# Decoder layer, one core: the low parts of the projected context made by GpSimd instead of VectorE, and three biases folded elsewhere

## The reference

```python
# 1: relative-position attention over T=8, 16 heads of 32
qkv = x @ in_proj_weight.T + in_proj_bias             # q, k, v
p = (pos @ pos_proj_weight.T + pos_proj_bias)         # per head
ac = einsum('tbhd,sbhd->bhts', q + r_w_bias, k)
bd = rel_shift(einsum('tbhd,rhd->bhtr', q + r_r_bias, p))[..., :t]
ctx = einsum('bhts,sbhd->tbhd', softmax((ac + bd) / sqrt(32)), v)
x = layernorm(x + ctx @ out_proj_weight.T + out_proj_bias)
# 2: cross attention, 8 heads of 64, over 512 context rows of width 1024
src_key, src_val = split((context @ W_src.T + b_src) * mask)
tgt = (x @ W_tgt.T + b_tgt) * mask
attn = softmax(where(mask == 0, -inf, tgt . src_key / 8))
x = layernorm(x + cat([x, attn . src_val]) @ W_out.T + b_out)
# 3: feed forward 512 -> 2048 -> 512 with values rounded to fp8/fp16
x = layernorm(x + quantized_ffn(x))
```

## Time and profile before

| | us |
|---|---|
| median of 3 runs | 1931.64 (1931.17 to 1934.32) |
| the profiled execution, its own time | 1929.76 |
| its span on the core | 1927.9 |
| first half | 0 to 820 |

### The profile page before, as it was taken

The page is one execution under the profiler, slowest core; times in us unless marked ns, Lnnn a source line. Parts: engine busy times, 40 slices in busy tenths (PEclk is TensorE's granted clock), DMA queues, the critical chain, the costliest instruction groups (busy, mean ns, idle before and its releaser), DMA issues. The chain is left out here.

```text
span 1927.9 us, 33302 instructions
## 1 busy us (share of the span) xinstructions
PE 1829.5 (95%) x12476; PEld 1003.3 (52%) x12476; DVE 1333.2 (69%) x1676; ACT 785.3 (41%) x1208; POOL 558.7 (29%) x576
## 2 busy tenths in 40 slices
PE   7999999999999989878899999999999999999998
PEld 3665465546554646445455454455454554554543
DVE  2899998999899998667465554655655646556521
ACT  3423222222222222248365363562653635626522
POOL 3135964786368345400102002003011020030010
PEclk9999999999999999979999999999999999999999
DMA  8436355425633566574413406207135052071010
GB/s 212 124 79 151 78 152 143 116 77 151 150 94 99 125 172 137 150 167 157 99 39 61 122 1 116 66 1 138 44 51 131 1 111 72 1 133 27 12 33 22
DMA packets 322654, 183.97 MB, mean 95 GB/s; under 512 B 225584, under 2 KB 278832, under 8 KB 322511
## 3 DMA queue, kind: packets, MB, share of 16 engines
q1 hardware_dynamic: 316448, 178.37, 38.9%
q10 hardware_dynamic: 6062, 3.49, 0.8%
HBM read 94.75 MB, written 33.55 MB: 67 GB/s over the span
## 5 line engine op out<-in xcount | busy, mean ns | idle before, releaser
L1531 DVE TENSOR_TENSOR p_lo<-k,p_hi 128x1024 f16<-128x1024 f32 x128 | 156.8, 1225 | 194.4 <-ACT p_hi L1404 194.4
L1176 POOL TENSOR_TENSOR q<-q,x_hi 128x512 f16<-128x512 f32 x28 | 37.6, 1374 | 638.7 <-ACT x_hi L1457 638.7
L1576 DVE CUSTOM_DVE_ANT_0 junk<-b_sx,mneg 128x512 f16<-128x512 f32 x256 | 175.9, 687 | 32.6 <-issue 23.2
L1204 PE MATMUL b_ff<-x2T_hi,w1T_hi 128*128 128x512 f16 x512 | 194.7, 380 | 1.9 <-DVE x2T_lo L1531 1.9
L1204 PE MATMUL b_ff<-x2T_lo,w1T_hi 128*128 128x512 f16 x512 | 194.7, 380 | 0.0
L1204 PE MATMUL b_ff<-x2T_hi,w1T_lo 128*128 128x512 f16 x512 | 194.6, 380 | 0.0
L1436 ACT ACTIVATE k<-b_st,mbias 128x512 f32<-128x512 f32 x256 | 161.9, 685 | 14.0 <-PE b_st L1250 13.4
L577 PE MATMUL sm_b<-cT_hi,wsT_hi 128*128 128x256 f16 x512 | 141.8, 277 | 15.2 <-DMA cT_lo<-rows_lo 13.6
L784 DVE TENSOR_TENSOR prod<-q,k 128x4096 f32<-128x4096 f32 x32 | 142.2, 4443 | 17.5 <-ACT q L660 16.7
L1404 ACT ACTIVATE p_hi<-k 128x1024 f16<-128x1024 f32 x128 | 135.3, 1057 | 45.5 <-PE b_av L1265 43.1
L1428 ACT ACTIVATE hq<-b_ff,b 128x512 fp8e4<-128x512 f32 x128 | 88.0, 687 | 155.6 <-PE b_ff L1204 149.0
(11 more groups left out here) (272 smaller groups left out, 4368.9 us busy)
## 6 DMA issues: line engine op xcount, KB each, us to landing
cn<-in_ctx_dram SPq DMA_DIRECT2D x64, 256.0 KB, 3.1
k<-kT_scratch SPq DMA_DIRECT2D x24, 512.0 KB, 7.7
x<-in_x_dram SPq DMA_DIRECT2D x32, 256.0 KB, 3.1
x_scratch<-x SPq DMA_DIRECT2D x32, 256.0 KB, 2.2
q<-x_scratch SPq DMA_DIRECT2D x8, 1024.0 KB, 5.6
q<-x_scratch SPq DMA_DIRECT2D x32, 256.0 KB, 2.9
out_dram<-q SPq DMA_DIRECT2D x32, 256.0 KB, 4.4
xn<-in_x_dram SPq DMA_DIRECT2D x24, 256.0 KB, 2.9
```

Of the source, the lines that this page charges most:

```text
L1204: mm = pe.matmul(out, a, c, start=(start and n == 0), stop=end)
L1531: dve.tensor_tensor(dst, bank, hi, ALU.subtract).then_inc(out, 1)
L1576: dve.tensor_tensor_reduce(junk[:, :], sx_b[tt % 2][:, :], mneg[:, :], 1.0, NEG, ALU.add, ALU.max, mx[:, h % 2, tt:tt + 1]).then_inc(s["sx ...
```

## The change

1. **Low parts of the context's quarters.** ACT makes two copies of each quarter in place of one: the fp16 high part as before, and the same scaled values in 32 bits (`stage_f`). PE's bank is free after ACT's second copy (`sm_copied`). POOL makes the low part from the two SBUF copies (over the first half of the 32-bit buffer); the instruction of DVE is gone. In POOL's program it stands behind the `o` row and ahead of the `x` and `c` rows of the step.
2. **Bias of k.** The 32 bias matmuls of the k projections are gone. The bias of k enters the position terms: `kb` holds it per head, is multiplied with q's biases in `position_bias` (8 small matmuls in place of 4) and added to `pb` before `position_weights`. Two more loads of a bias as a column at the start, small additions by DVE.
3. **Bias of the context's values.** The 32 bias matmuls of the value quarters are gone. At the start of the second half 12 matmuls with the value bias (`bv16`, 2 rows x 512 columns each) multiply it with the output weights, and DVE adds the result to the output bias. PE does them ahead of the first queries and waits for DVE's `step` to reach 7; one more load of 512 single elements is issued by ACT ahead of its copies.
4. Small things of the first half move into `ctx1`; `ones` is smaller; the first k projection no longer waits for the bias rows, the first q projection does.

```diff
@@ phase_a, buffers
-    stage = [pair(f"stage{i}", [P, 512]) for i in range(2)]
+    stage_f = [sb(f"stage{i}_f", [P, 512], F32) for i in range(2)]
+    stage = [[sb(f"stage{i}_hi", [P, 512], F16)[:, :], stage_f[i][:, :].bitcast(F16)[:, 0:512]] for i in range(2)]
@@ gpsimd
+            def stage_lo(n):
+                hi, lo = stage[n % 2]
+                pool.wait_ge(s["sm_copied"], n + 1)
+                pool.tensor_tensor(lo, stage_f[n % 2][:, :], hi, ALU.subtract).then_inc(s["sm_lo"], 1)
...
                 for use in plan.uses(g):
-                    row_lo(*use)
+                    if use[0] == "o":
+                        row_lo(*use)
+                for n in plan.quarters(g - 1):
+                    stage_lo(n)
+                for use in plan.uses(g):
+                    if use[0] != "o":
+                        row_lo(*use)
@@ tensor
             def position_bias():
-                pe.wait_ge(s["pb_ready"], 4)
+                pe.wait_ge(s["pb_ready"], 8)
                 for o in range(4):
-                    mm = pe.matmul(pos_b[0:2, 128 + o * 64:128 + (o + 1) * 64], bqr2[:, o, :],
-                                   pb[:, o, :, :].rearrange("p h r -> p (h r)"), start=True, stop=True)
+                    for z, terms_of in enumerate((pb, kb)):
+                        mm = pe.matmul(pos_b[0:2, 128 + o * 64:128 + (o + 1) * 64], bqr2[:, z, o, :],
+                                       terms_of[:, o, :, :].rearrange("p h r -> p (h r)"), start=(z == 0),
+                                       stop=(z == 1))
...
-                if (kind, i) == ("k", 0):
+                if (kind, i) == ("q", 0):
                     pe.wait_ge(s["step"], 5)
-                pe.matmul(out, ones, bias, start=False, stop=True).then_inc(s["pj_filled"], 1)
+                if kind != "k":
+                    mm = pe.matmul(out, ones, bias, start=False, stop=True)
+                mm.then_inc(s["pj_filled"], 1)
...
             def context_products(n):
                 if n >= 3:
-                    pe.wait_ge(s["sm_lo"], n - 2)
+                    pe.wait_ge(s["sm_copied"], n - 2)
...
-                    mm = pe.matmul(out[:, :], pick[:, BIAS["src_v"] + 1, :], rows[:, :], start=False, stop=True)
@@ scalar, stage_hi
-                act.activation(stage[n % 2][0][:, :], sm_b[n % 3][:, :], ACT.Copy, scale=scale).then_inc(s["sm_hi"], 1)
+                act.activation(stage[n % 2][0], sm_b[n % 3][:, :], ACT.Copy, scale=scale)
+                act.activation(stage_f[n % 2][:, :], sm_b[n % 3][:, :], ACT.Copy, scale=scale).then_inc(s["sm_copied"], 1)
@@ vector
-            def stage_lo(n):
-                scale = mks[(n // 4) % 2][:, n % 4 - 2:n % 4 - 1] if n % 4 >= 2 else 1.0 / WS
-                hi, lo = stage[n % 2]
-                dve.wait_ge(s["sm_hi"], n + 1)
-                dve.scalar_tensor_tensor(out=lo[:, :], in0=sm_b[n % 3][:, :], scalar=scale, in1=hi[:, :],
-                                         op0=ALU.mult, op1=ALU.subtract).then_inc(s["sm_lo"], 1)
@@ phase_b, tensor
             pe.wait_ge(s["wq_lo"], len(jobs))
+            pe.wait_ge(s["step"], 7)
+            products(ff_b[0][0:2, :], [t for j in range(KT) for t in terms([z[:, j, :] for z in bv16],
+                                                                           [z[:, KT + j, :] for z in wxT])],
+                     None, s["step"])
             queries_and_first_scores(0, None)
@@ phase_b, scalar
+                act.dma_start(bv[:, :], d.src_b[E:2 * E].rearrange("(o p) -> p o", p=P)).then_inc(s["cols_ld"], 16)
@@ phase_b, vector
             dve.tensor_scalar(raw[:, :], raw[:, :], WS, None, ALU.mult).then_inc(s["step"], 1)
-            dve.wait_ge(s["step"], 3)
+            for z in range(2):
+                dve.tensor_copy(bv16[0][:, :, z], bv[:, :]).then_inc(s["step"], 1)
+            dve.wait_ge(s["step"], 5)
+            for z in range(2):
+                dve.tensor_tensor(bv16[1][:, :, z], bv[:, :], bv16[0][:, :, z], ALU.subtract).then_inc(s["step"], 1)
+            dve.wait_ge(s["step"], 8)
+            dve.tensor_tensor(raw[:, :], raw[:, :], ff_b[0][0:2, :], ALU.add).then_inc(s["step"], 1)
```

More of the change, by code:

```diff
@@ L530, in projection @@
                     rhs = [z[:, :, a * E:(a + 1) * E] for z in winT]
-                    ones, bias, out = pick[:, BIAS[kind], :], rows[:, :], pj_b[n % 3][:, :]
+                    ones, bias, out = None if kind == "k" else pick[:, PICK[kind], :], rows[:, :], pj_b[n % 3][:, :]
                 if i == 0:
@@ L557, in output_projection @@
                         pe.matmul(out, a, c, start=(j == 0 and m == 0), stop=False)
-                pe.matmul(out, pick[:, BIAS["out"], :], rows[:, :], start=False, stop=True).then_inc(s["om_filled"], 1)
+                pe.matmul(out, pick[:, PICK["out"], :], rows[:, :], start=False, stop=True).then_inc(s["om_filled"], 1)
             def context_products(n):
@@ L806, in softmax @@
                 dve.tensor_tensor(flat, flat, wide, ALU.subtract).then_inc(s["probs"], 1)
-                for part in plan.quarters(16 * b + 7):
-                    stage_lo(part)
                 dve.wait_ge(s["exped"], b + 1)
@@ L919, in _ @@
                     position_bias()
-                for n in plan.quarters(g - 1):
-                    stage_lo(n)
                 score_sums(0, g)
```

68 lines of the change are left out of this document (41 added, 27 removed).

## The result

The kernel before ran at 1931.4 us in this comparison, the changed kernel at a median of 1952.7 us (1945.6 to 1960.5): the ratio is 1.0109, with a 95% interval of 1.0069 to 1.0149. The forecast was 1924.4 us with a range up to 1940, so the change is slower where a gain was expected. The profiled execution of the changed kernel took 1945.61 us (span 1943.8) and is the shortest of the four; its times are read against the 1929.76 us (span 1927.9) of before, 15.9 us apart.

What follows compares the result with a forecast made beforehand. PE was taken as the bound of the first half, DVE a close second. Terms -13.5 + 1.5 + 0 + 4.8 = -7.2 us from 1931.64 gave 1924.4 us; range 1912.5 to 1940.

Steps and rivals of the forecast that it cites:

- POOL's low part: First half: 64 new POOL instructions, contending with DVE and delaying `c` rows, cost +1.5 us, bounds -9 and +15.
- in value steps the `c` rows come one to two instructions later, 1.15 to 2.3 us: POOL's queue in value steps: low parts ahead of the `c` rows delay them by 1.15 to 2.3 us each time.
- DVE gets 71 us back, so it should still stay behind PE: First half: DVE's 71 us of relief outweighs up to 64 x 1.0 us of contention with POOL.
- POOL paces: Rival, last batch's value steps: POOL's work exceeds PE's 13.3 us a step, costing 15 us; 1938 us, chance 0.20.
- Bias matmuls: First half: 64 fewer bias matmuls on PE, a few small ones added; net -13.5 us if PE stays the bound.
- The relief of DVE: First half: DVE loses 44.7 us of work and 26.3 us of waits, which pays nothing directly.
- its rival at -9: Rival: most of PE's last-batch holes and part of its 13.6 us of waits close, -9 us; 1914 us, chance 0.12.
- ACT's second copy: First half: 64 further copies of 0.59 us fit into ACT's idle time; cost 0, at most 0.6 us once.
- Start of the program: Before ACT's first copy: two more column loads and small DVE instructions cost 0, bounds 0 to 1.5 us.
- Head: Start of second half: load issue 0.8, DVE's steps 1.4, twelve matmuls 2.6; together +4.8 us, bounds 4.0 and 9.6.
- moved, not lengthened: Start of second half: PE's existing low-clock stretch only shifts, so the twelve matmuls cost 2.6 us, not 5.1.
- the signs listed: Checks on matmul counts, step lengths (3.3 us shorter), DVE, POOL, `cT_lo` waits and head; growth limits would show it wrong.

Runs made afterwards that it cites:

- a_bias: Kernel before with parts 2 and 3 of the change alone; low parts stay on DVE, ACT copies once: 1931.6 us, ratio 0.9998.
- h_zero: Changed kernel without POOL's low parts; ACT's second copy writes zeros in their place: 1922.7 us, ratio 0.9955.
- e_dummy: a_bias plus 64 POOL subtractions whose result nobody reads, at the places of the changed kernel's low parts: 1951.1 us, ratio 1.0091.
- k_head: a_bias with the value bias split before DVE's fifth weight job and multiplied during `x1T`'s low parts, loads in their order: 1937.2 us, ratio 1.0020.
- k_head2: a_bias with the value bias's load issued ahead of the two other column loads and split after DVE's last weight job: 1929.0 us, ratio 0.9976.

## Why the prediction was wrong

As balance of the 21 us, from the ratios times 1931.4: bias matmuls and head together 0 (a_bias), that is -4 to -6 and +4 to +6; DVE's relief with ScalarE's second copy -8 (h_zero less a_bias); POOL's low parts +30 (changed kernel less h_zero).

*POOL's low part, "+1.5 us, bounds -9 and +15".* This is the step that failed, and by most: it measured +30 us, and +18 where nobody waits for them (e_dummy). The parts of the mechanism were read rightly from the earlier trace rows: the turns, the price of 1.15 us, who waits behind. Two terms were mis-sized. First, "in value steps the `c` rows come one to two instructions later, 1.15 to 2.3 us": between two of DVE's two-input instructions POOL gets one instruction in, so one place in the queue costs up to one DVE instruction, 2 to 5 us; five of POOL's took 16.85 us and one wait of PE 15.6. Second, "DVE gets 71 us back, so it should still stay behind PE": the 26.3 us of waits were no work, and what each turn puts on DVE falls into the value steps, where the earlier trace rows had it at 82.3 of 84 us. There DVE gained nothing: 84.98 busy us for 82.27. The relief came out in the score steps alone: 382 us in all against the 389 of a_bias, while the value steps are 376 against 353.

The rival "POOL paces" named this mechanism, its place and its sign, and its price of 15 us was half of what it measured. It should have been the forecast. Its own condition, POOL's work of a step above PE's 13.3 us, could have been worked out, and was met (16.85 us for five of them): four factor instructions, one `o`, two `c`, two low parts, each but the factors blocked until one of DVE's four instructions ends. The count of places, five for four gaps, was in its text, and the argument against it, that blocked instructions cost nobody, leaves out that DVE is blocked as well. The Trainium skill, page "SBUF — State Buffer", section "Who interferes with whom", calls the ports that the two engines share an exclusive lock, for which a VectorE instruction with two SBUF inputs contends with a GpSimd instruction that reads SBUF. The trace of the changed kernel agrees, with POOL's two `cn` rows of 6.89 us around DVE's product of 5.26 us, from 720 to 727.

*Bias matmuls, "net -13.5 us, if PE stays the bound".* The condition failed. The matmuls went (64 in the group, 0.215 us each), and 4 to 6 us came out; with DVE relieved it was 7.6, not clearly more; and 27.5 us more of PE's time gave 3.7. In the earlier trace rows both engines are at 98% in the value steps. I read that as "PE is the bound, DVE a close second" and gave PE's saving in full; the runs fit another reading, that with two engines at the bound the smaller of the two savings is what comes out, and DVE had none there.

*The relief of DVE, "pays nothing directly", and its rival at -9.* It paid 8 us in h_zero, near the rival's number, but by luck: the rival had it in PE's holes of the last batch, and h_zero's value steps there are 97 us as before; its gain is in the score steps, 378 us against the 389 of a_bias. In the changed kernel POOL took it back. *ACT's second copy, "cost 0":* right, it is within the -8. *Start of the program:* the first score product began no later than before (49.2 us, before 51.5).

*Head, "+4.8 us".* Right: 5.8 to the first query, 4.1 to the end of the first 24. ACT's issue took 0.90 us (0.8 forecast), DVE's steps some 1.2 (1.4 forecast), the products 4.2 for 2.6; and that the stretch at the low level is "moved, not lengthened" held as well, since the queries behind are all at the high level.

Of the signs listed, those for the counts held (64 matmuls, POOL's mean of 1.665 us, L829's above 2.514). Batch against batch the steps were to be 3.3 us shorter and were 2 us longer. The waits for `cT_lo` were 28.7 us and not at most 18.6, 15.1 more than before, and ACT's first copy behind the barrier came at 834.49 where it was at 824.18, not 8 us earlier: these two had been named as what would make the prediction wrong.

## What to carry to other kernels

When two engines are each busy 98% of a stretch, as here, don't count a saving on one of them in full: it is worth no more than the other can give too. Before work goes to GpSimd beside a VectorE that runs two-input instructions back to back, count places, not microseconds: here GpSimd got one instruction in per VectorE instruction, each pushed VectorE back by some 0.8 us too, and everything in its queue moved by a whole VectorE instruction. If such work is moved at all, the score steps, where every other VectorE operation is a reduction that reads one operand, were the place where it cost nothing; nothing measurable came of it either. And look at the head of a phase for loads: ask what a wait counts, and put it where the last of the loads has landed.

## What the runs showed of the hardware beyond that

- 64 GpSimd subtractions that nobody reads cost 18 us of kernel time, at 1.57 us each and 1.15 free.
- A load of 512 single elements landed 12.5 us after its issue when a load of 2048 and one of 512 single elements stood ahead of it in the queue (k_head), and 3.2 us when it was first (k_head2). The last of the others then took 3.94 us to issue instead of 2.39.
- A PE program shorter by twelve matmuls ran 36 us slower: stops of up to 4.2 us for "issue" in the second half, 21.6 us in all, and 0.5 us with twelve idle products in their place. The cause was not shown. For an experiment that takes out instructions this means that one kernel with as many idle ones in their place belongs beside it.
- Medians of one kernel and its single profiled execution differ by up to 7 us here (1952.7 and 1945.6 us), so terms under 2 us were taken from stretches, not from spans.
